# First attention's score products on 64-row halves of one packed k stack, with the list of steps redrawn

## The reference, cut to what matters

```
qkv = (xin @ Wqkv.T + qkv_bias).reshape(Bs, Lx, 3, H, D)
...
qn = q / jnp.maximum(jnp.linalg.norm(q, axis=-1, keepdims=True), 1e-12) * sm
kn = k / jnp.maximum(jnp.linalg.norm(k, axis=-1, keepdims=True), 1e-12)
scores = jnp.einsum('bhqd,bhkd->bhqk', qn, kn) + attn_bias
p = jax.nn.softmax(scores, axis=-1)
o = jnp.einsum('bhqk,bhkd->bhqd', p, v)
```

## Time and profile before

| what | value |
|---|---|
| time, median of 3 runs | 268.54 us (267.06 to 268.93) |
| profiled execution, its span | 266.0 us |
| PE busy | 232.5 us, 1,710 matmuls |
| DVE busy | 202.7 us, 421 instructions |
| ACT busy | 154.9 us, 303 instructions |
| POOL busy | 117.4 us, 184 instructions |

### The profile page before, as it was taken

How to read it: one execution, slowest core, us unless ns; L and a number is a source line. 1 busy time by engine, 2 the same in 40 slices (tenths; PEclk the granted TensorE clock), 3 DMA queues, 4 the chain that set the end, 5 groups by cost and what they waited for, 6 DMA issues and landing times.

```text
span 266.0 us, 4823 instructions
## 1 busy us (share of the span) xinstructions
PE 232.5 (87%) x1710; PEld 186.4 (70%) x1710; DVE 202.7 (76%) x421; ACT 154.9 (58%) x303; POOL 117.4 (44%) x184
## 2 busy tenths in 40 slices
PE   0679788978998899899949999999998899989992
PEld 0658545736775678667738999999995767778682
DVE  4378969598994797797584486778799999997742
ACT  2301593447798898857894976811914564646520
POOL 8767973146062200801969237128226595650000
PEclk9999999599999999999999999999999999999999
DMA  5990000000800000000041000000000000001012
GB/s 172 374 276 0 4 1 0 0 1 3 315 5 7 1 2 5 2 0 5 2 122 33 11 1 2 0 0 2 0 2 1 0 5 0 0 2 39 0 42 79
DMA packets 8248, 10.11 MB, mean 38 GB/s; under 512 B 1824, under 2 KB 7072, under 8 KB 8224
## 3 DMA queue, kind: packets, MB, share of 16 engines
q1 hardware_dynamic: 8224, 9.79, 11.1%
HBM read 8.61 MB, written 1.05 MB: 36 GB/s over the span
## 4 chain that ended last, share of the span: by engine, by line
PE 51%; DVE 16%; ACT 11%; issue 8%; POOL 7%; DMA 3%; SPq 2%; ACTq 0%; DVEq 0%; POOLq 0%
PE ring L785 8%; PE ring L786 7%; PE ring L787 7%; PE ring L791 6%; PE ring L838 5%; PE psx L863 5%; PE pv L883 4%; DMA xs<-in_x 3%; PE ring L1047 3%; DVE nm L1153 3%; ACT kstk L673 3%; ACT kstk L672 2%; PE pv L1062 2%; ACT ps L598 2%; POOL nt L450 1%
## 5 line engine op out<-in xcount | busy, mean ns | idle before, releaser
L1153 DVE TENSOR_REDUCE nm<-ring 128x2 f32<-128x512 f32 x64 | 40.2, 683 | 5.3 <-PE ring L838 5.2
L598 ACT ACTIVATE ps<-psx 128x1024 f32<-128x1024 f32 x32 | 31.3, 1026 | 7.5 <-PE psx L863 4.3
L838 PE MATMUL ring<-kstk,qstk 128*128 128x512 f32 x64 | 25.0, 449 | 4.1 <-ACT kstk L673 2.7
L785 PE MATMUL ring<-wqkv_hi,xm_hi 128*128 128x512 f32 (+1 forms) x64 | 24.3, 379 | 4.4 <-DVE xm_lo L1146 2.9
L786 PE MATMUL ring<-wqkv_lo,xm_hi 128*128 128x512 f32 (+1 forms) x64 | 23.3, 364 | 0.0
L787 PE MATMUL ring<-wqkv_hi,xm_lo 128*128 128x512 f32 (+1 forms) x64 | 22.9, 358 | 0.0
L838 PEld LDWEIGHTS ring<-kstk,qstk 128*128 128x128 f32 x64 | 11.3, 193 | 13.9 <-DVE nm L1153 5.3
L791 PE MATMUL ring<-ident,stack 128*128 128x128 f32 x128 | 17.7, 278 | 2.9 <-ACT kstk L673 1.4
L863 PE MATMUL psx<-qstk,kstk 128*128 128x256 f32 x128 | 19.7, 287 | 0.3 <-ACT ps L598 0.3
L863 PEld LDWEIGHTS psx<-qstk,kstk 128*128 128x128 f32 x128 | 17.8, 189 | 2.5 <-ACT ps L598 0.9
L883 PE MATMUL pv<-ps,vs 128*32 128x256 f32 x256 | 16.1, 383 | 3.6 <-issue 3.3
(11 more groups left out here) (195 smaller groups left out, 695.6 us busy)
## 6 DMA issues: line engine op xcount, KB each, us to landing
xs<-in_x SPq DMA_DIRECT2D x4, 256.0 KB, 8.2
stage_a<-in_wada SPq DMA_DIRECT2D x4, 256.0 KB, 6.9
stage_a<-in_wfc SPq DMA_DIRECT2D x1, 1024.0 KB, 5.0
stage_b<-in_wfc SPq DMA_DIRECT2D x1, 1024.0 KB, 8.7
out<-x SPq DMA_DIRECT2D x4, 256.0 KB, 2.1
row<-in_rows SPq DMA_DIRECT2D x1, 906.0 KB, 8.8
stage_b<-in_wqkv SPq DMA_DIRECT2D x1, 768.0 KB, 7.0
stage_a<-in_wqkv SPq DMA_DIRECT2D x1, 768.0 KB, 4.5
```

The lines of the kernel that those rows point to most:

```text
L598: a.activation(ps[:, n % 4], psx[:, n % 2], ACT.Exp).then_inc(exp_done, 1)
L785: mm(dst, lhs[0], rhs[0], start=start, stop=False)
L838: last = mm(dst, qstk[:, b % 2, p, qc * P:(qc + 1) * P], kstk[:, b % 2, 2 * p:2 * p + 2, :], start=True, stop=not with_bias)
L1153: v.tensor_reduce(nm[:, qc, :, p], bank(key).rearrange("p (h n) -> p h n", h=2), AX.X, ALU.max, negate=True).then_inc(ring_dve, 1)
```

## The change

The k stack is packed like the q stack, two heads to a tile of 128 rows, without zeros. A product for one head takes 64 rows of the k tile and the same 64 rows of the q tile (`head_rows`). A max step makes four matmuls of 256 columns in place of two of 512: it claims two ring banks, one for each head of the pair, before the first of them, and alternates between the halves. A score step still has four matmuls of 256 columns, now alternating between the halves, each half with a bank of its own. A copy of a turned k bank is one instruction in place of two. The two fills with zeros and the wait for them are gone. The freed half of the stack becomes a buffer `w1_sb` for fc1's weights, so `split_w1` waits for no scores any more; fc2's weights take the k stack. The maxima are ordered by head pair instead of by half of the queries.

The list is redrawn from end to end. Among the moves: `gamma_rows` now stands ahead of the first turned tiles; `unit0:2`, `qk0:3` and `v0:2` stand behind `max0:1.0` instead of ahead of it; `split_w1` stands among the maxima of the fourth batch (behind `max0:3.3`) instead of behind them; `split_wqkv1` stands ahead of the first `fc1`. The two `zeros` steps are gone; all other steps are the same.

```diff
     if name == "max0":
-        return [(("mx", b, q // PAIRS, q % PAIRS), "dve") for q in (2 * i, 2 * i + 1)]
+        return [(("mx", b, i, par), "dve") for par in range(2)]
...
-        kstk = sb("kstk", [P, 2, H0, L], F32R)
+        kstk = sb("kstk", [P, 2, PAIRS, L], F32R)
+        w1_sb = sb("w1_sb", [P, 2, 2048], F32R)
...
-        w1_hi = kstk[:, 0, 0:8, :].rearrange("p a b -> p (a b)").rearrange("p (f n) -> p f n", f=FC)
-        w1_lo = kstk[:, 0, 8:16, :].rearrange("p a b -> p (a b)").rearrange("p (f n) -> p f n", f=FC)
-        w2_hi = kstk[:, 1, 0:8, :]
-        w2_lo = kstk[:, 1, 8:16, :]
+        w1_hi, w1_lo = (w1_sb[:, k, :].rearrange("p (f n) -> p f n", f=FC) for k in range(2))
+        w2_hi, w2_lo = kstk[:, 0], kstk[:, 1]
...
-                if name == "zeros":
-
-                    g.memset(kstk[:, b, :, :].bitcast(F32), 0.0).then_inc(kzero_ready, 1)
...
-                    if i_ == 0 and b < 2:
-                        act.wait_ge(kzero_ready, b + 1)
                     if i_ == 0 and b >= 2:
                         act.wait_ge(s_full, PAIRS * (b - 1))
                     for u in range(2):
                         key = ("kT", t, u)
                         act.wait_ge(*full(key))
-                        src = bank(key).rearrange("p (a n) -> p a n", a=4)
-                        dst = kstk[:, b % 2, :, i_ * P:i_ * P + P].rearrange("p (a c) n -> p a c n", c=2)[:, 4 * u:4 * u + 4]
-                        a.activation(dst[0:SLOT, :, 0, :], src[0:SLOT], ACT.Copy)
-                        a.activation(dst[SLOT:P, :, 1, :], src[SLOT:P], ACT.Copy).then_inc(ring_act, 1)
+                        a.activation(kstk[:, b % 2, 4 * u:4 * u + 4, i_ * P:i_ * P + P],
+                                     bank(key).rearrange("p (a n) -> p a n", a=4), ACT.Copy).then_inc(ring_act, 1)
...
                 if name == "split_w1":
 
-                    act.wait_ge(s_full, 3 * PAIRS)
...
-            def max_scores(b, qc, p, with_bias):
-
-                key = ("mx", b, qc, p)
-                dst = claim(key)
-                if (qc, p) == (0, 0):
+            def head_rows(par):
+
+                return slice(SLOT * par, SLOT * par + SLOT)
+
+            def max_scores(b, p, with_bias):
+
+                if p == 0:
                     for w in ("qT", "kT"):
                         pe.wait_ge(*emptied((w, TB * b + 1, 1)))
-                last = mm(dst, qstk[:, b % 2, p, qc * P:(qc + 1) * P], kstk[:, b % 2, 2 * p:2 * p + 2, :],
-                          start=True, stop=not with_bias)
...
+                dst = [claim(("mx", b, p, par)) for par in range(2)]
+                for qc in range(TB):
+                    for par in range(2):
+                        rows_ = head_rows(par)
+                        last = mm(dst[par][:, qc * L:(qc + 1) * L], qstk[rows_, b % 2, p, qc * P:(qc + 1) * P],
+                                  kstk[rows_, b % 2, p, :], start=True, stop=not with_bias)
...
+                        if qc == TB - 1:
+                            last.then_inc(ring_full, 1)
...
-                for i in range(2):
-                    for kc in range(TB):
+                for kc in range(TB):
+                    for i in range(2):
                         keys = slice(kc * P, kc * P + P)
-                        last = mm(dst[:, i, kc, :], kstk[:, b % 2, 2 * p + i, keys], qstk[:, b % 2, p, :],
+                        last = mm(dst[:, i, kc, :], kstk[head_rows(i), b % 2, p, keys], qstk[head_rows(i), b % 2, p, :],
                                   start=True, stop=not with_bias)
...
-                v.tensor_reduce(nm[:, qc, :, p], bank(key).rearrange("p (h n) -> p h n", h=2), AX.X, ALU.max,
+                v.tensor_reduce(nm[:, :, par, p], bank(key).rearrange("p (q n) -> p q n", q=TB), AX.X, ALU.max,
                                 negate=True).then_inc(ring_dve, 1)
```

More of the change, by code:

```diff
@@ L81 @@
[L81 to L110, removed]
@@ L111 @@
-heads1_lo:2 heads1:2 turnp1:3.0 turnp1:3.1 root1:3 heads1_lo:3 proj1:2 value1:3 proj1:3 cos:3.1 heads1:3
+silu stats0:0 norm0:0 const_sel const_v ada split_wqkv0 split0:0 normed0:0 qk0:0.0 head_scales const_stack
+stats0:1 qk0:0.1 square0:0.0 square0:0.1 normed0:1 stats0:2 norm0:1 sums0:0 root0:0 norm0:2 split0:1 square0:1.0
+square0:1.1 ada_rest stats0:3 v0:0 bias_count root0:1 normed0:2 unit0:0.0 unit0:0.1 qk0:1.0 qk0:1.1 v0:1 lo0:0.0
+lo0:0.1 flag mask hi0:0.0 hi0:0.1 gamma_rows turnk0:0.0 turnq0:0.0 turnq0:0.1 turnk0:0.1 square0:2.0 square0:2.1
@@ new lines @@
+gamma:0 sums0:1 root0:2 gamma:1 norm0:3 split0:2 square0:3.0 square0:3.1 max0:0.0 max0:0.1 max0:0.2 max0:0.3
+gamma:2 gamma:3 unit0:1.0 unit0:1.1 max0:0.4 lo0:1.0 qk0:2.0 qk0:2.1 xbias0:0 hi0:1.0 hi0:1.1 max0:0.5 lo0:1.1
+turnk0:1.0 max0:0.6 max0:0.7 turnq0:1.0 turnq0:1.1 sums0:2 turnk0:1.1 root0:3 neg0:0 shift0:0 normed0:3 max0:1.0
+max0:1.1 score0:0.0 score0:0.1 max0:1.2 v0:2 split_wproj max0:1.3 split0:3 score0:0.2 score0:0.3 value0:0.0
+max0:1.4 value0:0.1 take0:0.0 score0:0.4 score0:0.5 unit0:2.0 max0:1.5 qk0:3.0 score0:0.6 max0:1.6 score0:0.7
@@ new lines @@
+unit0:2.1 qk0:3.1 max0:1.7 value0:0.2 value0:0.3 hi0:2.0 hi0:2.1 neg0:1 lo0:2.0 lo0:2.1 shift0:1 take0:0.1
+turnq0:2.0 out0:0.0 sums0:3 turnq0:2.1 turnk0:2.0 turnk0:2.1 out0:0.1 score0:1.0 max0:2.0 score0:1.1 max0:2.1
+score0:1.2 score0:1.3 max0:2.2 heads0:0 score0:1.4 score0:1.5 max0:2.3 heads0_lo:0 value0:1.0 max0:2.4
+value0:1.1 unit0:3.0 unit0:3.1 max0:2.5 take0:1.0 proj0:0 score0:1.6 score0:1.7 max0:2.6 hi0:3.0 lo0:3.0
+xbias1:0 value0:1.2 max0:2.7 neg0:2 value0:1.3 hi0:3.1 turnq0:3.0 lo0:3.1 shift0:2 turnk0:3.0 turnk0:3.1
@@ new lines @@
+score0:3.6 proj0:2 score0:3.7 stats1:2 split_w2 split_wqkv1 normed1:1 split1:0 out0:3.0 norm1:2 value0:3.2
+take0:3.1 value0:3.3 fc1:0.0 fc1:0.1 fc1:0.2 xbias0:3 out0:3.1 fc1:0.3 heads0:3 split1:1 normed1:2 heads0_lo:3
+gelu:0.0 gelu:0.1 gelu:0.2 fc1:1.0 fc1:1.1 proj0:3 gelu:0.3 gelu:1.0 gelu:1.1 split_wout1 fc1:1.2 fc1:1.3
+stats1:3 norm1:3 split1:2 fc2:0 xbias1:3 gelu:1.2 stats2:0 norm2:0 normed1:3 gelu:1.3 fc1:2.0 fc1:2.1 fc1:2.2
+fc1:2.3 split1:3 gelu:2.0 split2:0 gelu:2.1 normed2:0 gelu:2.2 gelu:2.3 fc2:1 stats2:1 norm2:1 rsums1:0
@@ L974, in walk @@
                     if name == "max0":
-                        for q in (2 * i_, 2 * i_ + 1):
-                            max_scores(b, q // PAIRS, q % PAIRS, with_bias)
+                        max_scores(b, i_, with_bias)
                     if name == "shift0":
@@ L1297, in _ @@
                 if name == "max0":
-                    for q in (2 * i_, 2 * i_ + 1):
-                        row_max(b, q // PAIRS, q % PAIRS)
+                    for par in range(2):
+                        row_max(b, i_, par)
                 if name == "neg0":
```

36 lines of the change are left out of this document (23 added, 13 removed).

## The result

The changed kernel takes 285.03 us (median of 4 runs, 284.28 to 286.15) against 268.74 in the same comparison: ratio 1.063, 95% interval 1.058 to 1.069. The profiled execution spans 282.5 us against 266.0.

What follows compares the result with a forecast made beforehand. VectorE was taken to be late next in the maxima, once products and k copies shrink. Terms of -1.2, -6.6, -2.1 and 0 took the 266.0 us span to 256.1; with 2.5 carried, 258.6 us, range 253 to 267.5.

Steps and rivals of the forecast that it cites:

- The price of the products: Max and score products: 0.118 us a pair of 64-row matmuls, 0.235 a step, saving 15.2 us of TensorE.
- halves one after the other: Rival: the paired 64-row matmuls run in sequence, so no product is saved; 265.7 us, chance 0.05.
- 42.1 to 120.5 ... I take 92%: First to last maximum, 78.4 us: VectorE's share rises from 84% to 92% over 66.1 us of work, giving 71.8, -6.6.
- maxima run dry: Rival: a max step claiming two of three ring banks leaves VectorE without maxima; 272.5 us, chance 0.11.
- After 141.7: no operation changes, the steps are redrawn. I take 0: After the first attention's last values, 124.3 us: no change from redrawn steps, bounds -3 and +3 us.
- Start to 42.1 ... -1.2: Start to first row maximum: two k copies fewer on the chain, -1.2 us, bounds 0 and -3.
- 120.5 to 141.7: -1.7 ... -1.8: Last maxima to last values: moving split_w1 up removes a TensorE stall (-1.7) and slow subtraction (-1.8); stretch -2.1 us.
- The clock: Sign against the forecast: the granted clock, 0.87 in the first stretch, falls in others too as TensorE gets lighter.

Runs made afterwards that it cites:

- e7: Changed kernel with the step order of before, each max step claiming one bank, making one head's products and handing it over before the other head: 265.3 us, ratio 0.989.
- e1: Changed kernel's products, copies and buffers with the step order of the kernel before: 271.6 us, ratio 1.016 to the kernel before.
- e8: Changed kernel with its redrawn list up to the last score and the old order from there: 276.7 us, ratio 1.032 to the kernel before.
- e11: e7 with one move of the new list, split_w1 placed among the fourth batch's maxima: 269.0 us, ratio 1.003 to the kernel before.
- e5: Changed kernel with the step order of before, each max product issued twice: 274.6 us, ratio 1.023 to the kernel before.
- e6: Changed kernel with the step order of before, max products run over all 128 rows, summing two heads: 271.4 us, ratio 1.013 to the kernel before.

## Why the prediction was wrong

**The price of the products** held: 0.12 a pair, 0.24 a step, changes of shape near 0.2, copies of k 16 at 0.61. The rival "halves one after the other" is out.

**"42.1 to 120.5 ... I take 92%"** failed. VectorE's share is 69.6 of 83.5 us (16.86 + 38.40 + 14.38), 83%, as before; its busy time is 3.5 us more than the 66.1 that I held fixed, 2.3 of them in the subtraction for the heads beside GpSimd's (3.02 in place of 0.69). What the share could reach was shown by e7: 74.9 us (41.9 to 116.8) in place of 78.4, a gain of 3.5 at a share of 88%.

**The rival "maxima run dry"**, at 0.11, had the cause and nearly the size, but not the form. It decided at 8 us dry, and the claim of two banks costs some 6 us in the maxima on the old list (0.027 by the ratios) and some 3 on the new. I set it low because "the list puts units, sums and splits between the maxima"; but those fill VectorE, not the ring. VectorE did not run dry. Its waits for max products between 42 and 150 us (total, times, longest), before, in the changed kernel, in e1 and in e7:

```profile
DVE nm L1153 <- PE ring L838: 5.2, 4, 3.9
...
DVE nm L1149 <- PE ring L834: 5.0, 11, 0.8
...
DVE nm L1147 <- PE ring L832: 6.6, 8, 2.2
...
DVE nm L1146 <- PE ring L832: 2.6, 3, 1.9
```

They came oftener, which the prediction named as a sign, but hardly grew. What grew is TensorE's wait for a bank, 10.9 us in the changed kernel and 13.0 in e1, in turns of 1.35 us a step, and that stands on the chain.

**"After 141.7: no operation changes, the steps are redrawn. I take 0"** and **"Start to 42.1 ... -1.2"** failed: +4.3 and +4.6. Together they are the largest mistake. I priced the list's named moves and took the rest as neutral, with bounds of 3 us, while each engine walks it in order. By the runs the list makes 0.047 of the loss of 0.063 (e1). Between the profiled executions of e1 and the changed kernel, 11.5 us apart, it is 3.6 up to the first maximum, 2.3 in the maxima and 5.7 behind the first gelu. For the tail e8 shows it (0.032); for the start no run takes the order and the clock apart.

**"120.5 to 141.7: -1.7 ... -1.8"** failed in sign: +2.5. The subtraction that took 2.46 beside GpSimd was read rightly, but moving GpSimd's part earlier moved the meeting to a place where VectorE bounds (e11, on the old list).

**The clock** I named as a sign only, and gave it no rival. It fell for 37.5 us in place of 6.8. On the old list e5 and e6 had 10 and 14 us less of it than e1 and were no faster, but their max steps were dearer, so its price is not taken apart. Its share in the new list is not settled.

## What to carry to other kernels

Before counting a faster product, count the buffers that its step claims at once against those that exist: two of three leave no stock, and a slower step that hands over bank by bank was some 6 us better on the same list. A list that every engine walks in order is a change of its own; time the new operations on the old list first, and price a redrawn stretch by its own run, not at nothing. When a GpSimd pass is moved, look which VectorE instructions it will now run beside.

## What the hardware did that was not expected

VectorE's subtraction beside a long GpSimd instruction ends at a fixed distance behind it, however early it began: 133.68 against 133.13 us in the earlier trace rows, 115.82 against 115.27 in e11, 129.90 against 129.37 in e7, and in the changed kernel's fourth batch 122.84 + 3.02 = 125.86 against 120.76 + 4.55 = 125.31, by these rows:

```profile
120.76 4.55 POOL L512 TENSOR_TENSOR w_sb<-stage_a,w_sb 128x2048 fp32r<-128x2048 f32 x1 [6.09 <-ACT w_sb L564]
...
121.63 1.29 DVE L1149 TENSOR_REDUCE nm<-ring 128x2 f32<-128x512 f32 x2 [0.66 <-PE ring L834]
122.84 3.02 DVE L1189 TENSOR_TENSOR at_lo<-stage_a,at_hi 128x512 fp32r<-128x512 f32 x1
```

0.53 to 0.55 us each time, though 2.46, 3.98, 2.90 and 3.02 us long: that fits a wait for the other's end, not a slower pace. The Trainium skill (SBUF — State Buffer, SBUF: two separate sides) has the ports that the two engines share as an exclusive lock for a whole instruction, where the loser fully blocks. These rows agree. The row maxima, which read PSUM, were not held up beside the same pass: two took 1.29 us at 121.63. In the profile such a wait counts as busy time, so VectorE's 76% hides it: its group of norms has 11.0 us in the changed kernel and 3.3 in e1, for the same eight instructions.

```profile
L1132 DVE TENSOR_SCALAR xh<-x,mv,rstd 128x256 f32<-128x256 f32 x8 | 11.0, 1413 | 1.4 <-POOL rstd L439 0.8 <-PE ring L781 0.6
```

```profile
L1130 DVE TENSOR_SCALAR xh<-x,mv,rstd 128x256 f32<-128x256 f32 x8 | 3.3, 460 | 0.6 <-POOL rstd L437 0.6
```
